# Low halves, kept tokens, a split wait and earlier class values in a wavelet-and-attention tower on one Trainium2 core

## What is computed

```python
h = _L0_tok_ref(x, Wa, ba, Wd1, bd1, Wd2, bd2, Wd3, bd3)          # wavelet, gates, inverse
h = concatenate([cls_tok, h], axis=1)                             # 257 tokens
h = h + attn(layernorm(h), ...)      # 4 layers:
    # qkv = h @ W_qkv; kr = r @ W_r
    # prob = softmax(((q + u) k^T + (q + v) kr^T) / sqrt(64))
    # h = ln1(h + (prob @ v) @ W_o); h = ln2(relu(h @ W_ff1 + b) @ W_ff2 + b)
h = h + moe(layernorm(h), ...)
```

## Time and profile before

| | us |
|---|---|
| median of three runs | 2518.98 |
| profiled execution | 2520.23 |
| its span, first to last instruction | 2518.4 |
| token stage, to the start of the second block | 139.27 |
| second block to the first score of round 0 | 46.1 |

### The profile page before, as it was taken

How to read it: one execution, slowest core, us unless ns; L and a number is a source line. 1 busy time by engine, 2 the same in 40 slices (tenths; PEclk the granted TensorE clock), 3 DMA queues, 4 the chain that set the end, 5 groups by cost and what they waited for, 6 DMA issues and landing times.

```text
span 2518.4 us, 61172 instructions
## 1 busy us (share of the span) xinstructions
PE 2224.4 (88%) x19318; PEld 1661.3 (66%) x19318; DVE 1848.3 (73%) x5687; ACT 1601.8 (64%) x4853; POOL 1190.4 (47%) x2205
## 2 busy tenths in 40 slices
PE   0249999999989999999989999999899999988998
PEld 0127777777767777777767777777677777765665
DVE  8837777777767777777757777777678888886543
ACT  2217777777767777776757777776667777665322
POOL 3015555555456555554545555554565555541211
PEclk9679999999999999999999999999999999999999
DMA  5354444445554444444644444455533343355110
GB/s 167 84 147 105 122 102 112 112 109 149 154 146 121 108 110 110 109 123 141 187 125 117 112 102 116 105 149 148 158 97 93 100 107 97 98 146 185 52 47 22
DMA packets 378059, 295.35 MB, mean 117 GB/s; under 512 B 45087, under 2 KB 350721, under 8 KB 376739
## 3 DMA queue, kind: packets, MB, share of 16 engines
q1 hardware_dynamic: 370603, 272.41, 41.4%
q10 hardware_dynamic: 4864, 12.68, 1.5%
q0 software_dynamic: 2272, 6.35, 0.7%
HBM read 137.71 MB, written 72.07 MB: 83 GB/s over the span
## 4 chain that ended last, share of the span: by engine, by line
PE 36%; ACT 23%; DVE 13%; POOL 7%; issue 6%; SPq 5%; DMA 4%; DVEq 0%; POOLq 0%; ACTq 0%
ACT e_rows L2162 11%; PE bk L2064 5%; PE bk L2076 5%; PE bk L2033 4%; PE bk L1279 4%; PE bk L1905 4%; ACT pt L2147 4%; SPq L1538 3%; DVE x L2419 3%; DVE o_rows L2327 2%; ACT rel L2097 2%; PE bk L1893 2%; PE bk L1844 2%; POOL arena L1732 2%; POOL arena L1730 2%
## 5 line engine op out<-in xcount | busy, mean ns | idle before, releaser
L2162 ACT ACTIVATE e_rows<-e_rows,nb 128x257 f32<-128x257 f32 x1024 | 516.4, 515 | 47.7 <-DVE nb L2356 47.1
L2356 DVE CUSTOM_DVE_ANT_0 e_rows<-bk,arena 128x257 f32<-128x257 f32 x1024 | 390.1, 418 | 81.2 <-PE bk L1938 79.8
L1844 PE MATMUL bk<-hin,arena 128*128 128x257 f16 x3072 | 424.9, 276 | 18.2 <-DMA hin<-hd_dram 8.8
L2318 DVE TENSOR_TENSOR pt<-bk,pt 128x512 f16<-128x512 f32 x512 | 353.7, 691 | 64.4 <-ACT pt L2147 51.6
L1893 PE MATMUL bk<-ident,e_rows 128*128 128x128 f32 x2048 | 324.1, 281 | 49.5 <-ACT e_rows L2162 28.2
L1732 POOL TENSOR_TENSOR arena<-rel,arena 128x257 f16<-128x257 f32 x496 | 328.3, 662 | 41.4
L1844 PEld LDWEIGHTS bk<-hin,arena 128*128 128x128 f16 x3072 | 298.5, 98 | 69.6 <-issue 17.1
L1730 POOL TENSOR_SCALAR arena<-rel 128x257 f16<-128x257 f32 x496 | 203.6, 410 | 273.0 <-ACT rel L2097 264.9
L2147 ACT ACTIVATE pt<-bk 128x512 f16<-128x512 f32 x512 | 310.2, 606 | 7.2 <-PE bk L1893 7.2
L1893 PEld LDWEIGHTS bk<-ident,e_rows 128*128 128x128 f32 x2048 | 221.5, 141 | 135.1 <-ACT e_rows L2162 113.0
L1937 PE MATMUL bk<-arena 128*128 128x257 f16 x1024 | 256.7, 275 | 11.7 <-DMA arena<-arena 11.2
(11 more groups left out here) (329 smaller groups left out, 4181.7 us busy)
## 6 DMA issues: line engine op xcount, KB each, us to landing
arena<-arena SPq DMA_DIRECT2D x768, 128.5 KB
wf<-in_w_dram SPq DMA_DIRECT2D x168, 128.0 KB, 2.9
w_split_dram<-wh SPq DMA_DIRECT2D x168, 128.0 KB, 2.3
xs_dram<-in_c_blank_dram SPq DMA_DIRECT2D x24, 772.5 KB
wf<-in_we_dram SPq DMA_DIRECT2D x96, 128.0 KB, 2.7
we_split_dram<-wh SPq DMA_DIRECT2D x96, 128.0 KB, 2.0
w_rest<-w_split_dram SPq DMA_DIRECT2D x12, 1024.0 KB, 17.2
arena<-we_split_dram SPq DMA_DIRECT2D x8, 1536.0 KB, 12.3
```

Of the source, the lines that this page charges most:

```text
L1844: r_ = mm(bank[4 + s % 2][:, 0:S], wcol(a, C_QKV, k, 3 * HD, chunk_at(s)), hin[:, m, k, :], start=i == 0, stop=i == 5)
L2162: act.activation(E[:, h % EB, qt, :], E[:, h % EB, qt, :], ACT.Exp, bias=nb[:, 2 * h + qt:2 * h + qt + 1], scale=-1.0, accum_out=sums[:, q ...
L2318: v.tensor_tensor(pt[:, h, 1, :, 0:IMG], bank[2 + h % 2][:, :].rearrange("p (k s) -> p k s", k=QT), pt[:, h, 0, :, 0:IMG], ALU.subtract).t ...
L2356: v.tensor_tensor_reduce(E[:, h % EB, qt, :], bank[qt][:, 0:S], cb[:, h, :], -SCORE, 3e38, ALU.add, ALU.min, nb[:, 2 * h + qt:2 * h + qt + ...
```

## The change

Four parts.

1. *Token stage, weights.* VectorE makes all seven low halves, GpSimd none. Chunks come in the order 5, 6, 3, 0, 1, 2, 4. ScalarE centres 5 and 6: eight accumulating passes over 256 columns, a scaling, eight passes with a bias, per chunk. The high half is one pass for every chunk, where it was two for chunks 0 to 3. VectorE makes six low halves where it made three (ahead of the layer norm) and the seventh behind it. ScalarE issues loads 3 to 5 after the exponential, load 6 after the high half of the fourth chunk.
2. *Tokens kept on chip.* `hs` lies in `p_flat`, the attention stage's probability buffer. `hd` is still stored, but nobody waits at the block's end; the first `hin` is copied on chip; SyncE waits for the store before the second `hin`, ScalarE before round 0 writes probabilities.
3. *Round 0 and waits.* TensorE's class values don't wait for GpSimd's memsets; the position load moves behind query copy 4. The wait for 24 stacking DMAs is split: 12 before head 0, 12 before head 8, in every round.
4. *Entry rounds.* Normalisation and gain of both halves at head 4 on GpSimd, low halves at 6 and 7 (high halves on ScalarE at 6 and 7), class values at heads 9, 10 and 11.

```diff
-        wd = [sb("wd_l1", [P, 384, 3]), sb("wd_l2", [P, 96, 3]), sb("wd_l3", [P, 24, 3])]
+        wd = [p_flat[:, 8224:8224 + 2304].bitcast(F32).rearrange("p (n k) -> p n k", k=3), sb("wd_l2", [P, 96, 3]), sb("wd_l3", [P, 24, 3])]
...
-        hs = sb("hs", [P, B, 2, KC, S], F16)
+        hs = p_flat[:, 0:B * 2 * KC * S].rearrange("p (b t k s) -> p b t k s", b=B, t=2, k=KC)
...
+        CHUNKS = (5, 6, 3, 0, 1, 2, 4)
+        FIRST_CENTRED = C_O // 2048
...
-            sp.dma_start(io["hd"].rearrange("b p n -> p b n"), hs[:, :, :, :, :].rearrange("p b t k s -> p b (t k s)")).then_inc(hd_out, 16)
-            sp.wait_ge(hd_out, 16)
+            sp.dma_start(io["hd"].rearrange("b p n -> p b n"), hs[:, :, :, :, :].rearrange("p b t k s -> p b (t k s)")).then_inc(keep["hd_first"], 16)
...
-            for i in range(BY_POOL):
-                t, c = wst[:, i % NS, :], slice(i * 2048, (i + 1) * 2048)
-                pool.wait_ge(w_hi, i + 1)
-                pool.tensor_tensor(w_part(W, 1, c.start, c.stop), t, w_part(W, 0, c.start, c.stop), ALU.subtract).then_inc(w_lo, 1)
...
+                act.wait_ge(w_lo, i - NS + 1)
...
+            def centre_weights(i):
+
+                act.wait_ge(w_in[i % NS], 16 * (i // NS + 1))
+                t = wst[:, i % NS, :].rearrange("p (j c) -> p j c", c=SPLIT)
+                for j in range(CJ):
+                    act.activation(t[:, j, :], t[:, j, :], ACT.Identity, accum_out=wmean[:, i, j:j + 1]).then_inc(w_sum, 1)
+                act.wait_ge(w_sum, (CJ + 1) * i + CJ)
+                act.activation(wmean[:, i, :], wmean[:, i, :], ACT.Copy, scale=-1.0 / SPLIT).then_inc(w_sum, 1)
+                act.wait_ge(w_sum, (CJ + 1) * (i + 1))
+                for j in range(CJ):
+                    act.activation(t[:, j, :], t[:, j, :], ACT.Identity, bias=wmean[:, i, j:j + 1]).then_inc(w_centred, 1)
...
+            for i in range(2):
+                centre_weights(i)
             for i in range(NS):
                 weights_hi(i)
-            load_weights(NS)
-            weights_hi(NS)
-            load_weights(NS + 1)
-            load_weights(NS + 2)
             act.wait_ge(logit_ok, 1)
             act.activation(e[:, :, :], z[:, :, :], ACT.Exp).then_inc(exp_ok, 1)
-            load_weights(NS + 3)
-            weights_hi(NS + 1)
+            for i in range(NS, 2 * NS):
+                load_weights(i)
+            weights_hi(NS)
+            load_weights(2 * NS)
+            for i in range(NS + 1, 2 * NS):
+                weights_hi(i)
...
-            for i in range(BY_POOL, NW):
+            for i in range(2 * NS):
                 split_weights(i)
 
             v.wait_ge(h0_in, 16 * 5)
             layer_norm_rows(v, step, xt, xt, stats, mv, rstd, var_ok, y0_ok)
             v.sem_inc(xn_ok, 1)
+            split_weights(2 * NS)
...
-            sp.dma_start(flat(hin), io["hd"][0]).then_inc(hin_in, 16)
+            sp.dma_start(flat(hin), p_flat[:, 0:2 * KC * S]).then_inc(hin_in, 16)
...
+            sp.wait_ge(hd_first, 16)
             load_hin(0)
...
+                        early = kind.entry
+                        if not early and h in (4, 5):
                             ln2_normalise(at, h - 4)
...
+                        if early and h == 4:
+                            for k in range(KC):
+                                ln2_normalise(at, k)
+                            for k in range(KC):
+                                ln2_gain(at, k)
+                        if h in ((6, 7) if early else (9, 10)):
+                            ln2_lo(at, h - (6 if early else 9))
...
-            pe.wait_ge(const_ok, CONST)
             first = At(pe, 0)
             class_v()
+            pe.wait_ge(const_ok, CONST)
...
-                pe.wait_ge(stack_in, at(384, 384))
                 for h in range(H):
+                    if h in (0, NP):
+                        pe.wait_ge(stack_in[h // NP], at(192, 192))
...
-                    if h == NP + 3 and kind.entry:
+                    if h == NP + 1 and kind.entry:
...
-            load_position_term(first)
             for s in range(0, 2 * NP, 2):
                 take_q(first, s)
+                if s == 4:
+                    load_position_term(first)
...
+                if at.g == 0:
+                    act.wait_ge(hd_first, 16)
+                    act.wait_ge(hin_in, 16)
```

## The result

| | before | after |
|---|---|---|
| median of the runs, us | 2518.59 (2516.37 to 2522.68, 4 runs) | 2495.62 (2493.25 to 2499.14, 4 runs) |
| profiled execution, us (its span) | 2520.23 (2518.4) | 2493.25 (2491.4) |
| mean granted clock | 0.978 | 0.986 |

The ratio is 0.9904, with a 95% interval of 0.9892 to 0.9917: about 24 us less, where 30.0 had been forecast (2518.98 to 2489.0). The two profiled executions differ by 27.0: the profiled one of after is also its fastest, and that of before lies 1.6 above its median.

The account below looks back on a forecast made before the run. It took a chain of engines feeding each other through 32 attention rounds as the bound, and looked at the single-file start: 7.6 + 7.8 + 16.1 - 1.5 = 30.0 off, 2489.0 us in the median, range 2478 to 2503.

Parts of the forecast that it names:

- Dot products, reconstruction: Start, part 1: low halves moved to VectorE end the dot products at 45.6 instead of 61.0, 15.4 off.
- Layer norm: Start, part 1: begins at 98 instead of 105.6, 7.6 off, bounds 2.2 and 15.4; loads in full cost 13.2.
- I take 98, past the middle: Layer norm's start, chosen between 90.2 (untouched by loads) and 103.4 (all four paid in full).
- a fourth load that nearly misses the tokens: Token trip: the last weight load, issued near 84, may find the tokens nearly in; reason for stopping short of 103.4.
- (a): Token trip: loads fit between token packets, layer norm starts near 90, 8 more off, 2481; chance 17%.
- (c): Token trip: loads run in series, 12.2 each, layer norm at 113, 15 less off, 2504; chance 7%.
- Tokens kept: Part 2, end of the token stage: SyncE's wait for stored hd goes, 7.8 off, bounds 6 and 8.
- First round: Part 3, attention's first round: first score at about T+30 against T+46.1, 16.1 off, bounds 10 and 18.
- issued by T+25.5 (9.72): First round: the first stack, starting at T+15.8, takes 9.72 to issue and lands by T+28.5.
- Rival (b): First round: position load or hin, sharing with hd and the stack, holds the start to T+34 to T+36; 2494; 15%.
- 5.6 for the moved position load: First round: position load behind query copy 4 brings the first query copy at T+7.7 instead of T+13.3.
- Entry rounds: Part 4, first rounds of layers 1 to 3: +0.5 each, 1.5 on in all, bounds -17 and +9.

Follow-up runs that it names:

- the joint wait: Changed kernel with the wait for both stacks ahead of head 0 again in every round: 2503.96 us, ratio 0.9949.
- the entry order: Changed kernel with the entry rounds' normalisation and class values back at their earlier heads: 2496.47 us, ratio 0.9906.
- six executions of the same program up to it: Profiles of the changed kernel and five kernels differing from it only in entry-round order; their first scores came at T+30.75 to T+33.71.
- seven buffers: Changed kernel with seven weight staging buffers instead of three, all weight loads issued at the start, none in the token trip: 2484.76 us, ratio 0.9869.
- the first order that removed it: Changed kernel with SyncE storing class values and reloading vbd ahead of the first stack in entry rounds: 2503.8 us, ratio 0.9926.
- seven kernels compared here: The kernel before, the changed kernel and five variants of its entry-round order, compared by an entry round plus the next; six had 140.7 to 143.7 us.

## Why the prediction was right, and where it was off

The mechanism held in every part, with the sizes off in two places, the tokens' trip and the first stack. Against after, at the mark in round 1, giving GpSimd its low halves back costs 6.1, waiting for `hd` 10.45, the joint wait 9.8, the position load 0.8 and the entry order nothing: 27.1, beside 26.3 between before and after. That these meet so closely is luck: the mark stands between 222.5 and 226.5 in the six executions of the same program up to it, so each difference can be some 4 off. By the ratios of whole runs the same five come to 34 against 24, each of them uncertain by 4 or 5.

- **Dot products, reconstruction:** 14.9 off for 15.4. ScalarE was through with centring at 31.6 and with three high halves at 37.0, under the dot products, as costed and with room to spare: an accumulating pass comes every 0.40, since its activation (0.40) and its read (0.19) overlap, so two chunks took 13.6 in place of at most 19.8.
- **Layer norm:** the first step that failed in size. "I take 98, past the middle" gave 7.6 off, and 4.9 came. Bounds and mechanism were right: 90.2 without loads (90.7 with seven buffers), 103.4 in full, and 100.6 measured; the experiment prices the loads at 9.9 of the 13.2. The 13.2 itself was right (13.1 of the engines' time); what was taken off it was too much. The reason given for stopping short, a fourth load that nearly misses the tokens, was weak: it was issued at 86.6, 14 before the tokens were in. Rivals (a) and (c), 90 and 113, didn't occur; seven buffers reached (a)'s time, but by having no load there, not by fitting loads in. The Trainium skill's rule that the prediction had set beside its sum ("DMA: Bandwidth & Descriptors", Issuing engines are not separate DMA queues) had given it 102.3 as an estimate; the measured 100.6 lies 1.7 from that and 2.6 from the 98, so the trace agrees with the rule in the main: three quarters of what the loads on ScalarE's queue took of the engines was paid in time.
- **Tokens kept:** T stood 25.67 behind layer norm, 33.71 before: 8.0 off for 7.8, and the experiment returned the 7.8 to the tenth.
- **First round:** T+31.0 for T+30. The terms inside were less good than their end. The first stack started at T+14.4, 1.4 sooner than forecast, and took 13.57 to issue instead of 9.72; "issued by T+25.5 (9.72)" is the term that failed. The prediction let the stack delay the position load, by up to 9.7, and not the load the stack: the load was in at T+23.9, sooner than the T+27 to T+29 it was given, and the stack paid. With the same program that issue is 13.3 to 16.4, the score T+30.8 to T+33.7, on average T+32.0. The profile pair of before and after had a good draw of it, which is part of why the medians differ by 23 and the profiles by 27. Rival (b), T+34 to T+36, lies just beyond the 33.7; its cause, the position load sharing with the stack, is what the traces show. The prediction's 5.6 for the moved position load was next to no gain: with the load in front the stack starts 5.7 later and is issued 4.3 faster. Of the 15.2 off at the first score the joint wait returns 11.9 and the position load 1.8; for the other 1.5 (class values ahead of the memsets, the first `hin` on chip) there is no run.
- **Round 0:** 1.8 of the 28.1 was lost by round 1, which the sum didn't have. From the first score to that mark it is 66.5 in after and 64.7 in before. About half of it is standing (3.1 idle on TensorE against 2.3; the wait of 1.28 for `hin` behind head 0 is new), and half the clock: the same 550 matmuls take 63.3 at a mean granted clock of 0.95, where before has 62.4 at 0.97. At 157 to 165, around that wait, the clock stood at 0.55.
- **Entry rounds:** +0.4 in three pairs for +1.5. The order of values ready and SyncE late was read rightly, and the row of before sufficed for it. The lower bound of 17 off was never in reach of the orders tried: it counted the wait as removable, and the first order that removed it made three pairs 11 longer.

Together: 4.9 + 8.0 + 15.2 = 28.1, less 1.8, less 0.4, plus the 1.1 by which all other rounds and the end differ (not traced), gives the 27.0 of the pair where 30.0 was forecast. Of the 6.6 between 2489.0 and 2495.62, 3.0 is in those terms. The rest is that the profiled execution of after lies 2.4 below its median, while the step from profile to median had taken the 1.25 of before, with the other sign.

## What to carry to other kernels

Work that is moved off a busy path takes its DMAs along: look at which stretch becomes empty (here 35 to 68, DMA share 0.00) and load there, before you accept transfers in a window that already shows 0.95. A wait on a DMA counts as a gain only when the queue and the engines behind it have been followed to the next round; of the seven kernels compared here six had sums within 3 of one another, whatever they waited for. And where a stack of copies is issued in a row, take its issue time from several executions, since the first thing behind it inherits all of its spread.

## What the runs showed of the hardware

- Twelve copies of 128.5 KB, issued in a row by SyncE, take 9.3 and 9.7 where a 2 MB load on ScalarE's queue overlaps them by 2.6 and 4.2, and 13.3 to 17.0 where it overlaps them by 9.3 to 13.1; in one program they lie up to 3.0 apart from one execution to the next. Four copies of 512 KB take 6.2 with no load beside them and 13.5 beside four loads of 1 MB. The profile shows this as issue time of the engine, not as a wait; that the queue is full then is my reading, and no row says it.
- Four loads of 1 MB, put into a token trip that had the DMA engines at 0.95, took 13.1 of the engines' time and made the trip 9.9 longer: 187 GB/s for the trip alone, 251 to 260 with the loads in it.
- VectorE's products with two inputs in SBUF took 3.9 to 4.6 beside each of GpSimd's subtractions (0.15 to 0.7 beside none), whether these stood at 23.0 as in before or at 36.2.
